# Selective scan in one block: halves one behind the other, float32 row tiles, the sum built turned, the norm merged in

## The reference

```
dt = softplus(x W_dt + b_dt)          [token, 128]
B = x W_B,  C = x W_C                 [token, 16]
for n in 0..15, per feature d, along the 512 tokens of a sequence:
    h_n[t] = exp(-exp(A_log[d,n]) dt[t]) * h_n[t-1] + dt[t] x[t] B[t,n]
    y[t]  += h_n[t] * C[t,n]
y += D_param * x
X = layernorm(X + y)
```

## Time and profile before

| | |
|---|---|
| median of 3 runs | 1778.8 us |
| the profiled execution | 1779.27 us, of which its span (first to last instruction) 1777.5 us |
| busy share of the span | PE 84%, DVE 60%, ACT 36%, POOL 12% |
| the scan stage, first product to last copy | 400.34 to 505.46 us |
| its loop, first scan to last product | 419.99 to 493.62 us |

### The profile page before, as it was taken

One profiled execution on the slowest core, in us unless ns is written; L12 is line 12 of the kernel. 1 busy time (PEld: TensorE's weight loads), 2 busy tenths in 40 slices (PEclk: granted clock), 3 DMA queues, 4 the chain that ended last, 5 costly groups with the idle time before them and its releaser, 6 DMA issues. The chain is left out here.

```text
span 1777.5 us, 22019 instructions
## 1 busy us (share of the span) xinstructions
PE 1499.6 (84%) x8172; PEld 686.7 (39%) x8172; DVE 1063.5 (60%) x2616; ACT 646.7 (36%) x936; POOL 217.7 (12%) x231
## 2 busy tenths in 40 slices
PE   2997889985777999998979998988988589996985
PEld 2232344431233344445433333354436323344353
DVE  6796454458946777754454972556455647755354
ACT  3465432224325033333424663422221245552431
POOL 3000010000000533331000000000000103331000
PEclk9898789998969999998987998998996679997788
DMA  5000000020000100000020000000010000000000
GB/s 207 1 1 1 1 1 0 1 104 35 1 0 1 48 1 1 1 1 1 1 78 26 1 1 1 1 1 1 0 72 1 1 1 1 1 1 1 1 1 12
DMA packets 4075, 27.16 MB, mean 15 GB/s; under 512 B 384, under 2 KB 2432, under 8 KB 2944
## 3 DMA queue, kind: packets, MB, share of 16 engines
q1 hardware_dynamic: 2912, 25.22, 3.6%
q10 hardware_dynamic: 1056, 0.52, 0.1%
HBM read 25.21 MB, written 0.52 MB: 14 GB/s over the span
## 5 line engine op out<-in xcount | busy, mean ns | idle before, releaser
L811 DVE TENSOR_REDUCE maxima<-banks 128x1 f32<-128x512 f32 (+4 forms) x640 | 363.1, 604 | 111.0 <-PE banks L660 104.3
L955 ACT ACTIVATE big<-banks 128x1024 f32<-128x1024 f32 (+2 forms) x320 | 294.3, 960 | 265.5 <-PE banks L703 94.2
L688 PE MATMUL banks<-big 32*128 32x512 f32 (+6 forms) x1280 | 232.6, 613 | 17.2 <-DVE big L832 12.9
L660 PE MATMUL banks<-big 32*128 32x77 bf16 (+6 forms) x1024 | 158.3, 297 | 23.5 <-ACT big L238 6.1
L1476 DVE TENSOR_TENSOR big<-big,banks 128x512 f32<-128x512 f32 (+1 forms) x116 | 79.7, 687 | 152.6 <-PE banks L1389 147.2
L724 PE MATMUL banks<-big,v_heads 128*9 128x512 f32 (+7 forms) x1024 | 159.6, 569 | 6.3 <-ACT heads_out L871 3.2
L477 POOL TENSOR_TENSOR rstd<-mean_var,minus_half 128x4 f32<-128x4 f32 x34 | 34.9, 1026 | 1033.9 <-DVE mean_var L399 1033.9
L1451 ACT ACTIVATE big<-banks 128x512 f32<-128x512 f32 (+1 forms) x116 | 69.1, 596 | 179.1 <-PE banks L1388 179.0
L660 PEld LDWEIGHTS banks<-big 32*128 32x128 bf16 (+1 forms) x1024 | 57.3, 97 | 182.0 <-DVE maxima L811 93.5
L1419 PE MATMUL banks<-big,moe_weights 128*128 128x512 f32 (+1 forms) x232 | 119.8, 601 | 3.0 <-ACT big L1459 2.6
L688 PEld LDWEIGHTS banks<-big 32*128 32x128 f32 (+3 forms) x1280 | 72.8, 178 | 70.3 <-ACT big L955 23.7
(11 more groups left out here) (410 smaller groups left out, 2216.5 us busy)
## 6 DMA issues: line engine op xcount, KB each, us to landing
moe_weights<-in_moe SPq DMA_DIRECT2D x1, 4864.0 KB, 14.5
moe_weights<-in_moe SPq DMA_DIRECT2D x1, 4768.0 KB, 22.5
moe_weights<-in_moe SPq DMA_DIRECT2D x1, 3264.0 KB, 10.5
moe_weights<-in_l3x SPq DMA_DIRECT2D x1, 3072.0 KB, 9.6
late_weights<-in_l2x SPq DMA_DIRECT2D x1, 2048.0 KB, 8.8
moe_weights<-in_l SPq DMA_DIRECT2D x1, 1234.0 KB, 13.1
rows<-in_rows SPq DMA_DIRECT2D x1, 1152.0 KB, 8.1
late_weights<-in_turned SPq DMA_DIRECT2D x1, 1152.0 KB, 16.9
```

The costliest lines, as they stand in the source:

```text
L660: last = nc.tensor.matmul(RING[n % NR][:, x * klen:x * klen + last_key(t)], q[rows, t * P:(t + 1) * P], ks[rows, 0:last_key(t)], start=Tru ...
L688: last = nc.tensor.matmul(SC[pair % 2][0:size, j % 2, n0:S], ks[rows, i * P:i * P + size], q[rows, n0:S], start=True, stop=turned)
L811: nc.vector.tensor_reduce(dst, src, AX_X, ALU.max).then_inc(ring_free.up(), 1)
L955: nc.scalar.activation(E[pair % NEP][0:size, :, n0:S], SC[pair % 2][0:size, :, n0:S], ACT.Exp, scale=scale).then_inc(exp_ready.up(), 1)
```

## The change

`layer1_scan` is rewritten as one block.

- dt's bias, minimum and maximum are taken by DVE straight from PSUM, each sequence for itself; ACT's Exp and Ln go over 512 tokens at a time.
- B and C are computed once, B on partitions 0 to 15 and C on 32 to 47 (`weights` is zero elsewhere), and are kept in float32: DVE copies sequence 0 and ACT sequence 1. The split into bf16 parts is gone. POOL alone makes `pick` (64 partitions, float32).
- Row n of B and of C are copied by two float32 products on 32 rows each (`rows`), into two pairs of banks in turn instead of three. The pair for step s+2 waits for ch(s).
- y is added up turned: for each 128 tokens ch is the loaded operand and the identity the streamed one (four products of 128 columns for one of 512), on top of a product of XT with diag(D). So no turning back and no D term are needed.
- The steps go through sequence 0 first, all 16 states, then sequence 1. `time_steps(1)` is done after step 2.
- The norm's sum and statistics of sequence 0 come after ch(17), its norm after ch(19), its transposes on PE after step 21, its moves on ACT after step 23. Those of sequence 1 follow the loop.

The core of the diff:

```diff
-    matmul_stream(c, halves(c, lambda half: [(c.m("L1_WdtT"), xnT[:, half * S:(half + 1) * S])], P, dtT, bias=c.col("L1_attn_b_dt")))
...
-            seq(dve, step, nc.vector.tensor_scalar(ex, dtT, -1.0, None, ALU.mult))
-            nc.vector.tensor_tensor(ex, ex, dtT, ALU.min).then_inc(z_ready.up(), 1)
-            seq(dve, step, nc.vector.tensor_scalar(mx, dtT, 0.0, None, ALU.max))
...
-            nc.vector.tensor_copy(bc[32:64, :], rest[32:64, :])
-            seq(dve, step, nc.vector.tensor_copy(mid[64:96, :], rest[64:96, :]))
-            nc.vector.tensor_tensor(bc[64:96, :], rest[64:96, :], mid[64:96, :], ALU.subtract)
...
-    steps = [(n, z) for n in range(N) for z in range(2)]
+    own = Norms(c, None, [Norm(c.X, turned=[(c.XT, None, None)])], c.X, sums=(6, 7), turned=(4, 5, 0, 1))
+    steps = [(n, z) for z in range(2) for n in range(N)]
+    def tile_products(z, src, right, start, stop):
+        for k in range(ST):
+            last = nc.tensor.matmul(c.bank[own.SUM[z]][:, k * P:(k + 1) * P], src[:, k * P:(k + 1) * P], right, start=start and k == 0,
...
-                if s >= 3:
-                    pe.wait_ge(ch_ready.sem, ch_ready.at(s - 2))
-                nc.tensor.matmul(BC[2 * (s % 3)][:, :], pick[:, n, :], x, start=True, stop=True)
-                nc.tensor.matmul(BC[2 * (s % 3) + 1][:, :], pick[:, N + n, :], x, start=True, stop=True).then_inc(in_ready.up(), 1)
+                if s >= 2:
+                    pe.wait_ge(ch_ready.sem, ch_ready.at(s - 1))
+                for j in range(2):
+                    rows = slice(32 * j, 32 * j + 32)
+                    last = nc.tensor.matmul(c.bank[2 * (s % 2) + j][:, :], pick[rows, n, :], bc[rows, zs[z]], start=True, stop=True)
+                last.then_inc(in_ready.up(), 1)
...
-                if s + 2 < len(steps):
+                pe.wait_ge(ch_ready.sem, ch_ready.at(s + 1))
+                if s < LAST - 1:
                     inputs(s + 2)
-                pe.wait_ge(ch_ready.sem, ch_ready.at(s + 1))
-                nc.tensor.matmul(YS[z][:, :], c.ident[:], ch[:, s % 2, :], start=(n == 0), stop=(n == N - 1)).then_inc(sum_ready.up(), 1)
+                done = own.sum_ready if n == N - 1 else summed
+                tile_products(z, ch[:, s % 2, :], c.ident[:], False, n == N - 1).then_inc(done.up(), 1)
+                if s == 21:
+                    own.turn_pair(pe, 0)
+                    own.turn_pair(pe, 1)
...
+            for z in range(2):
+                dve.wait_ge(dt_made.sem, dt_made.at(z + 1))
+                vector.tensor_scalar(ex[:, zs[z]], c.bank[z][:, :], c.col("L1_attn_b_dt"), 0.0, ALU.add, ALU.min)
+                vector.tensor_scalar(mx[:, zs[z]], c.bank[z][:, :], c.col("L1_attn_b_dt"), 0.0, ALU.add, ALU.max).then_inc(dt_read.up(), 1)
+                dve.wait_ge(dt_read.sem, dt_read.at(z + 1))
+                vector.tensor_tensor(ex[:, zs[z]], ex[:, zs[z]], mx[:, zs[z]], ALU.subtract).then_inc(abs_ready.up(), 1)
...
+                if s == 2:
+                    time_steps(1)
+                if s == 17:
+                    own.own_sum(dve, 0)
+                    own.own_stats(dve, 0, 0)
+                if s == 19:
+                    own.own_norm(dve, 0, 0)
...
-    norms(c, turned_back(c, yT), [Norm(c.X, turned=[(c.XT, None, None)])], c.X)
```

More of the change, by code:

```diff
@@ L299, with __init__ @@
     SUM, FRONT, TURNED = (2, 3), (4, 5), (0, 1, 6, 7)
-    def __init__(self, c, product, steps, base=None, row=None, total=None, front=None, weigh=None, store=None):
+    def __init__(self, c, product, steps, base=None, row=None, total=None, front=None, weigh=None, store=None, sums=None,
+                 turned=None):
         self.c, self.product, self.steps, self.front, self.weigh, self.store = c, product, steps, front, weigh, store
@@ L358, in pe_rest @@
         for pair in range(NT // 2 if final.turned else 0):
[L359 to L362 removed]
+            self.turn_pair(pe, pair)
         for half in range(2 if final.plain_turned is not None else 0):
@@ L368, in pe_rest, with turn_pair, move_pair @@
             last.then_inc(self.plain_turned.up(), 1)
+    def turn_pair(self, pe, pair):
+        c = self.c
+        pe.wait_ge(self.norm_ready.sem, self.norm_ready.at(pair + 1))
+        for k in range(2):
+            last = c.nc.tensor.transpose(c.bank[self.TURNED[pair]][:, k * P:(k + 1) * P], self.final.out[:, 2 * pair + k, :], c.ident[:])
+        last.then_inc(self.turned_ready.up(), 1)
+    def move_pair(self, queue, eng, pair):
+        c = self.c
+        queue.wait_ge(self.turned_ready.sem, self.turned_ready.at(pair + 1))
+        for dst, g, b in self.final.turned:
+            d, src = dst[:, 2 * pair * P:2 * (pair + 1) * P], c.bank[self.TURNED[pair]][:, 0:2 * P]
+            if eng is c.nc.vector:
+                copy_scaled(c, eng, d, src, g, b)
+            elif g is None:
+                eng.copy(d, src)
+            else:
+                eng.activation(d, src, ACT.Identity, bias=0.0 if b is None else b, scale=g)
     def scale(self, i, t):
@@ L498, in act_rest @@
         for pair in range(3 if final.turned else 0):
[L499 to L505 removed]
+            self.move_pair(act, scalar, pair)
         if final.plain_turned is not None:
@@ L1595, in layer1_scan @@
     ex, mx = c.big1(3 * TOK, TOK), c.big1(4 * TOK, TOK)
-    weights = c.big1(5 * TOK, 96).rearrange("p (k n) -> p k n", k=3)
-    bc, mid = (c.big1(6 * TOK + i * S, S)[0:96].bitcast(BF16) for i in range(2))
-    rest = c.big1(7 * TOK, TOK)[0:96]
-    pick = c.big3(0, N * P)[0:96].bitcast(BF16).rearrange("p (n m) -> p n m", n=2 * N)
+    bc = c.big1(5 * TOK, TOK)[0:64]
+    weights, diag = c.big1(6 * TOK, 64), c.big1(6 * TOK + 64, P)
+    pick = c.big3(0, N * P)[0:64].rearrange("p (n m) -> p n m", n=N)
@@ new lines, in layer1_scan @@
+    own = Norms(c, None, [Norm(c.X, turned=[(c.XT, None, None)])], c.X, sums=(6, 7), turned=(4, 5, 0, 1))
+    zs = [slice(z * S, (z + 1) * S) for z in range(2)]
+    steps = [(n, z) for z in range(2) for n in range(N)]
+    LAST = len(steps) - 1
+    def tile_products(z, src, right, start, stop):
+        for k in range(ST):
+            last = nc.tensor.matmul(c.bank[own.SUM[z]][:, k * P:(k + 1) * P], src[:, k * P:(k + 1) * P], right, start=start and k == 0,
+                                    stop=stop and k == ST - 1, skip_group_check=True)
+        return last
@@ L1677, in _ @@
         def _(act):
+            scalar.activation(c.negA, c.m("L1_A_log"), ACT.Exp).then_inc(neg_ready.up(), 1)
+            for z in range(2):
+                act.wait_ge(abs_ready.sem, abs_ready.at(z + 1))
+                last = scalar.activation(ex[:, zs[z]], ex[:, zs[z]], ACT.Exp)
+            seq(act, act_step, last)
+            for z in range(2):
+                scalar.activation(ex[:, zs[z]], ex[:, zs[z]], ACT.Ln, bias=1.0).then_inc(soft_ready.up(), 1)
+            act.wait_ge(bc_made.sem, bc_made.at(2))
@@ L1683, in _ @@
+            own.move_pair(act, scalar, 2)
         @block.vector
@@ L1690, in _ @@
+            dve.wait_ge(bc_made.sem, bc_made.at(1))
+            vector.tensor_copy(bc[:, zs[0]], c.bank[2][0:64, :]).then_inc(bc_dve.up(), 1)
+            time_steps(0)
             drive(0)
-            for s in range(len(steps)):
+            for s, (n, z) in enumerate(steps):
                 dve.wait_ge(driven.sem, driven.at(s + 1))
                 dve.wait_ge(a_ready.sem, a_ready.at(s + 1))
-                nc.vector.tensor_tensor_scan(h[:, s % 2, :], a[:, s % 2, :], bx[:, s % 2, :], 0.0, ALU.mult, ALU.add).then_inc(decay_used.up(), 1)
-                if s + 1 < len(steps):
+                vector.tensor_tensor_scan(h[:, s % 2, :], a[:, s % 2, :], bx[:, s % 2, :], 0.0, ALU.mult, ALU.add).then_inc(decay_used.up(), 1)
+                if s < LAST:
```

140 lines of the change are left out of this document (67 added, 73 removed).

## The result

| | before | after |
|---|---|---|
| median | 1779.09 us (1778.77 to 1780.36, 6 runs) | 1801.63 us (1797.63 to 1821.42, 6 runs) |
| the profiled execution | 1779.27 us | 1800.45 us |
| busy share of the span, PE / DVE | 84% / 60% | 86% / 59% |
| first scan, from the stage's first product | 19.65 us | 12.00 us |
| first scan to the last step's products | 73.63 us | 114.35 us |

The ratio after to before is 1.0157, 95% interval 1.0102 to 1.0211: slower, where no change was forecast. The medians differ by 22.5 us (1.3%). Of the six runs four lie from 1797.6 to 1802.4 and two at 1820.0 and 1821.4, which have no trace; the ratio follows the mean of all six, so these two raise it. In the profiled executions the stage grows from 105.12 to 133.20 us (+28.1); ahead of it 1.9 are won and behind it 5.0, in stretches whose instructions are the same. Inside the stage it is -7.6, +40.7 and -5.0.

A forecast was written before the change was run, and what follows sets the result against it. DVE was taken to set the pace, with PE having room. Terms -8.5 + 4.2 + 4.9 + 3.4 - 5.0 = -1.0 us gave a profiled 1778.3 and a median of 1777.8 us, no change; 8-in-10 range 1772 to 1788.

The forecast's parts named there:

- A, ahead of the loop: From the first product's reading to the first scan: scan at 411.5, -8.5 us, bounds -9.0 to -7.5.
- B, the first steps: First scan to ch(3): pairs wait for ch at the half clock, which rises by 419.7; +4.2 us.
- C, the steady steps: ch(3) to ch(30): turns of drive, ch and PE's pair take 2.49 against 2.31; 27 turns, +4.9 us.
- D, between steps: Sequence 0's sum, statistics, norm and transposes put between steps of the loop: +3.4 us.
- E, behind the loop: From the last ch's product to the last copy's end: 6.82 against 11.84, so -5.0 us.
- The second one: Loop: PE becomes the bound at the half clock, 1.4 more a step, seven steps, +9.8, 1787.6 us; chance 0.22.
- The fourth rival: Steady turn: each change of tile shape costs, 0.1 to 0.3 a turn, +3 to +8, about 1783 us; chance 0.12.
- The third: Pairs in the loop: the two row tiles do not run side by side, +23, 1801 us; chance 0.04.

The follow-up runs named there:

- 64-row version with one wait: The changed kernel with each pair's products on 64 rows, PE's own wait for ch dropped where the pair already waits: 1782.05 us, ratio 0.9997 to the kernel before.
- 64-row version: The changed kernel with C on partitions 64 to 79 and each of a pair's two products over 64 rows, added rows zero: 1779.85 us, ratio 1.0003.
- bf16 rows: The changed kernel with B and C again in three bf16 parts on 96 partitions, rows copied by two bf16 products: 1773.10 us, ratio 0.9951.
- four row tiles: The changed kernel with each 32-row pair preceded by two more 32-row products, zeros by zeros on rows 64 to 127: 1778.73 us, ratio 0.9992.
- three pairs of banks: The changed kernel with 64-row products and three pairs of banks in turn, the pair for step s+3 behind ch(s): 1775.17 us, ratio 0.9950.
- the first experiment: The changed kernel with seven more full-array products keeping PE busy up to the first ch: 1780.37 us, ratio 1.0026 to the kernel before.

## Why the prediction was wrong, step by step

**A, ahead of the loop: held.** From the stage's first product to the first scan 12.00 us, 11.2 foreseen; -7.6 against -8.5, inside its bounds. The difference is the clock: it was at 1.2 GHz up to 403, and the first product was read 2.09 behind its start (398.41 to 400.50) in place of 1.13 (400.34 to 401.47). From that reading on the chain took 9.91, 10.0 foreseen. ACT was late last, as said. POOL's copy came too early to disturb DVE; in the 64-row version with one wait, where it started 0.09 ahead of the first subtraction (402.51, 402.60), that took 2.34 in place of 0.69, a loss of 1.65 where up to 0.9 was feared.

**B, the first steps: the step that failed.** Its words were that the clock "falls as before, and rises some time after PE is at it again", by 419.7. It fell as foreseen (410.2) and rose at 502.4. I had carried over a rise seen with pairs on 96 rows and full products to a loop whose pairs use 64 of 128 rows; the two kernels that are the one before but for its pairs of rows (1830.86 on 32 rows each, 1776.25 on 64) show that this can't be done. The term put at +4.2, and everything behind it reckoned at 2.4 GHz, was to be reckoned at 1.2 GHz up to step 21. That lost 26.3 us against the 64-row version (below, the rivals).

**C, the steady steps: the mechanism right, two sizes off.** ch, pair, drive in a ring was right, and so were 0.68 for ch and 1.17 for the pair (1.16). PE's start was 0.15 and not 0.06, 0.08 of it from the doubled wait, which stands in the diff and was overlooked; drive to ch was 0.60 and not 0.58. That is 2.60 in place of 2.49, and with the wait dropped 2.52. Over 27 turns all of this would be worth 3 us. That the two row tiles run side by side (1.13 for the pair) holds.

**D, between steps: held, where the clock was up.** In the 64-row version with one wait the way from the first scan to the last products is 83.54 + 2.00 = 85.5 us (2.00 from the last scan to the last products, as 522.76 to 524.76 in the changed kernel); B, C and D together had foreseen 73.6 + 4.2 + 4.9 + 3.4 = 86.1. In that run the clock was back at 419.3, as B had assumed (419.7), so with B's assumption met the three terms add up. Sum and statistics took 2.1 of DVE (480.50 to 482.61), the norm 1.1. The power did meet a scan, but POOL gave way: from 482.78 it took 1.85 in place of 1.01, and the scan (482.61) kept its 1.22. What D lacked is that the insertion leaves PE idle, and that the clock can fall on it, as it did in four experiments (the one with products added ahead of the loop, the 64-row pairs, the one with products added behind step 4, and the bf16 rows). In three others (four row tiles, one wait, three pairs of banks) PE had the same 2.2 us without work and the clock stayed up.

**E, behind the loop: held.** 6.85 us, 6.82 foreseen.

**The rivals.** The second one is what happened: PE the bound at the half clock, 1.4 more a step (4.01 against 2.60), 3.9 foreseen for a step and 4.01 found. Its size was wrong: seven low steps, where the loop lost 112.35 - 86.06 = 26.3 us against the 64-row version, some 19 steps' worth. It had a chance of 0.22 and a time of 1787.6; with 19 steps it would have said 1804. The argument held against it, "PE is busier than in the loop before, which held the clock", is refuted by the window at 0.50 with PE busy for 89.34 of 92.10 us. The row that spoke for it, 27.2 us low with PE busy for 23.09, deserved more weight. The fourth rival falls as it was put, on the turn at the full clock: no price for a change of shape is left there once the second wait is gone. But in the low steps, where PE is the bound, the two changes cost 0.6 a step (2.00 and 2.01 against 1.70 and 1.71), an estimated 11 us of the 26.3 over 19 steps. They don't hold the clock down, since the 64-row pairs change shape as often. The page "TensorEngine Tiling (Array Packing)" of the Trainium skill (Key Properties) says that the change drains the engine; these 0.3 a change agree with it, and where PE has been idle, as ahead of each pair at the full clock, none of it is seen. The third falls with the 1.13; its 1801 is near the measured time by accident.

The page "TensorE: Matmul & The Clock Gate" of the Trainium skill (Part 1) ties the clock to how busy PE has been. The rows of the low loops (1.2 GHz with PE busy for 89.34 of 92.10 us and for 126.13 of 129.40) don't agree, if busy means that an instruction is at work; the measurement decides.

**Behind the stage.** The changed kernel got back 5.0 us there and the best versions lost some. The three windows are those of the changed kernel, the kernel before and the 64-row version with three pairs of banks, from the end of the last copy on:

```profile
531.70:1798.60 1266.90, 1099.36 (x6438) 521.94 (x6438) 724.82 (x1912) 460.04 (x671) 185.21 (x191) 0.90 0.02 9
```

```profile
505.50:1777.40 1271.90, 1104.20 (x6438) 523.24 (x6438) 725.37 (x1912) 459.73 (x671) 185.02 (x191) 0.90 0.02 9
```

```profile
498.20:1772.90 1274.70, 1107.61 (x6438) 524.57 (x6438) 724.69 (x1912) 460.21 (x671) 185.20 (x191) 0.89 0.02 9
```

The instructions are the same 6438; PE's busy time differs by 4.8 and 8.3 us and the length by 5.0 and 7.8, DVE's by less than 1. So it is most likely again the clock, met at other places; no run tested it. The stage's 7.2 us in the last version (105.12 to 97.95) shrink by 2.8 for that reason.

**Open.** What the two runs at 1820, the three long ones of the first experiment and the three at 1763.5 were, for want of a trace; what the chip measures in a product that uses half of the rows. Only pairs at rows 0 to 63 were run at 32 rows each, so whether the place of the idle rows matters wasn't tried.

## What to carry to other kernels

Before a product is made cheaper by using fewer rows of the array, ask what the loop is worth at the half clock: multiply PE's work in a step by two and compare it with the bound. If it is over, a low clock costs time in every step, and whether the loop gets out of it has to be measured with the new products, not carried over from the old ones. Rows of zeros may be the cheaper choice: pairs on 64-row tiles, 48 rows of each zero, took PE the same 1.13 and won 22 us here. In the low stretch each change of tile shape counts too. And a stretch in which another engine keeps PE idle has a price beyond its length where PE's share is close to the bound.

## What the runs showed of the hardware

- With float32 pairs on two 32-row tiles, 64 of 128 rows, a low clock did not come back by itself, though a high one was kept up to ch(17) (398.9 to 463.7). The clock stayed at 1.2 GHz for 92.1 us with PE busy for 89.34, and for 129.4 us with 126.13 in the kernel before with such pairs. With the same pairs on 64-row tiles, or with all four 32-row tiles at work, it was up for good at the latest 17 us after the first scan (414.2 to 431.1, four tiles), but for falls of 3.4 us at most.
- In such a loop four float32 products on all rows brought it back within 3 us (433.11 to 436.05).
- A wait on PE for a count that has been waited for is not free: 0.08 us a step (2.60 against 2.52, 64-row pairs).
- A change between row tiles and the full array behind busy work cost 0.3 us at 1.2 GHz (2.00 against 1.70 for the four products, 2.01 against 1.71 for the pair); behind an idle PE at 2.4 GHz nothing was seen (0.05 from ch to the pair).
- A VectorE instruction with both operands in SBUF and a GpSimd one held each other up, and the later one paid: GpSimd's power took 1.85 in place of 1.01 beside a scan that had started 0.17 before it (482.61, 482.78); VectorE's subtraction took 2.34 in place of 0.69 when GpSimd's copy of 1.89 had started 0.09 before it.
- Four 32-row products side by side take PE 1.14 (1.13 for two), so the added two cost at most 0.03 a step.
